# Fused cross-attention and FFN with LoRA on one core: the 4-byte passes of a head pair gathered into one group

## The reference

```python
def attention(hidden_q, hidden_kv, attention_mask, position_bias, Wq, Wk, Wv, Wo):
    q = (hidden_q @ Wq).reshape(b, lq, h, dh)      # b 16, lq 64, h 32, dh 128
    k = (hidden_kv @ Wk).reshape(b, lk, h, dh)
    v = (hidden_kv @ Wv).reshape(b, lk, h, dh)
    score = einsum('bqhd,bkhd->bhqk', q, k) * dh ** -0.5 + position_bias
    probs = softmax(where(mask, score, -inf)); probs = where(mask, probs, 0)
    return einsum('bhqk,bkhd->bqhd', probs, v).reshape(b, lq, h * dh) @ Wo
def ffn(x, ...):
    base_out = x @ base_W.T + base_b
    p = softmax(x @ router_W.T + router_b); w = the 8 largest of 15, summed by expert
    return base_out + (((x @ A.T) * w) @ B.T) * 2.0
x = x + attention(layernorm(x), ctx, mask, bias, Wq, Wk, Wv, Wo)
x = x + ffn(layernorm(x), ...)
```

## Time and profile before

| | |
|---|---|
| median of three runs | 833.14 us |
| profiled execution | 832.47 us |
| its span | 830.7 us |
| TensorE busy | 803.3 us, 97% |
| VectorE busy | 582.0 us, 70% |
| ScalarE busy | 341.0 us, 41% |
| GpSimd busy | 232.3 us, 28% |
| chain that ended last | TensorE 88%, VectorE 6% |

### The profile page before, as it was taken

How to read it: one execution, slowest core, us unless ns; L and a number is a source line. 1 busy time by engine, 2 the same in 40 slices (tenths; PEclk the granted TensorE clock), 3 DMA queues, 4 the chain that set the end, 5 groups by cost and what they waited for, 6 DMA issues and landing times.

```text
span 830.7 us, 16317 instructions
## 1 busy us (share of the span) xinstructions
PE 803.3 (97%) x6366; PEld 652.7 (79%) x6366; DVE 582.0 (70%) x1023; ACT 341.0 (41%) x657; POOL 232.3 (28%) x227
## 2 busy tenths in 40 slices
PE   8689999999999999969999999999999999998998
PEld 6578888888888888758888878888887878886786
DVE  4674435347677665588788888788787888758872
ACT  4544435245565554444334433344334433333410
POOL 0050404113424333253133322333133322111340
PEclk9789999999999999999999999999999999999999
DMA  6335665334454546564553436443563435442002
GB/s 215 99 142 169 231 224 178 114 130 163 153 177 153 176 148 203 193 188 135 153 176 112 141 108 179 134 145 106 152 178 112 137 110 152 122 150 38 1 9 93
DMA packets 108075, 118.35 MB, mean 142 GB/s; under 512 B 44240, under 2 KB 77008, under 8 KB 107999
## 3 DMA queue, kind: packets, MB, share of 16 engines
q1 hardware_dynamic: 107998, 117.31, 44.9%
HBM read 81.64 MB, written 35.65 MB: 141 GB/s over the span
## 4 chain that ended last, share of the span: by engine, by line
PE 88%; DVE 6%; ACT 2%; issue 1%; DMA 1%; POOL 0%; SPq 0%; ACTq 0%; DVEq 0%; POOLq 0%
PE pP L1253 38%; PE pY L1253 37%; PE pO L1433 4%; PE pS L1408 4%; PE pO L1253 2%; PE pT_ L1418 2%; DMA wk_raw<-in_L_xattn_Wq 1%; ACT wv_hi L624 1%; DVE co_lo L843 1%; PE pS L1299 1%; DVE oT_lo L843 0%; PE pT_ L1299 0%; DVE wk_lo L843 0%; DVE sums_c L887 0%; PE pO L1299 0%
## 5 line engine op out<-in xcount | busy, mean ns | idle before, releaser
L1063 DVE TENSOR_TENSOR y<-y,pY 128x512 f32<-128x512 f32 x124 | 84.4, 681 | 41.2 <-PE pY L1253 41.0
L1253 PE MATMUL pY<-wo_hi,oT_hi 128*128 128x512 f32 x248 | 97.8, 394 | 2.4 <-DVE y L1063 2.4
L1253 PE MATMUL pP<-xo_hi,wk_hi 128*128 128x512 f32 x224 | 97.2, 434 | 2.6 <-DVE q L853 1.7
L843 DVE TENSOR_TENSOR wk_lo<-twk,wk_hi 128x256 fp32r<-128x256 f32 x128 | 80.8, 643 | 23.7 <-ACT wk_hi L624 23.7
L1253 PE MATMUL pY<-wo_lo,oT_hi 128*128 128x512 f32 x248 | 96.8, 390 | 0.0
L1253 PE MATMUL pY<-wo_hi,oT_lo 128*128 128x512 f32 x248 | 96.5, 389 | 0.0
L1253 PE MATMUL pP<-xo_lo,wk_hi 128*128 128x512 f32 x224 | 88.7, 396 | 0.0
L1253 PE MATMUL pP<-xo_hi,wk_lo 128*128 128x512 f32 x224 | 88.4, 394 | 0.0
L547 POOL TENSOR_TENSOR bias<-bias,madd 128x512 f32<-128x512 f32 x32 | 42.0, 1313 | 139.5 <-DMA bias<-in_fside_Bx32xSxS 139.5
L624 ACT CAST wk_hi<-twk 128x256 fp32r<-128x256 f32 x128 | 52.1, 408 | 56.2 <-PE pP L1253 45.3
L843 DVE TENSOR_TENSOR wk_lo<-wk_raw,wk_hi 128x256 fp32r<-128x256 f32 x96 | 53.1, 553 | 20.9 <-ACT wk_hi L624 20.7
(11 more groups left out here) (256 smaller groups left out, 1887.5 us busy)
## 6 DMA issues: line engine op xcount, KB each, us to landing
v_hbm<-stage SPq DMA_DIRECT2D x64, 256.0 KB, 2.3
k_hbm<-stage SPq DMA_DIRECT2D x64, 256.0 KB, 3.2
k<-k_hbm SPq DMA_DIRECT2D x16, 1024.0 KB, 5.3
v<-v_hbm SPq DMA_DIRECT2D x16, 1024.0 KB, 6.1
wk_raw<-in_L_xattn_Wk SPq DMA_DIRECT2D x16, 512.0 KB, 4.5
wo_raw<-in_L_xattn_Wo SPq DMA_DIRECT2D x16, 512.0 KB, 3.7
bias<-in_fside_Bx32xSxS SPq DMA_DIRECT2D x128, 64.0 KB, 2.7
wk_raw<-in_L_xattn_Wq SPq DMA_DIRECT2D x16, 512.0 KB, 4.3
```

What stands on the lines that cost most here:

```text
L843: nc.vector.tensor_tensor(dst, src, hi.bitcast(F32), ALU.subtract).then_inc(done, 1)
L1063: nc.vector.tensor_tensor(y[:, t, :], y[:, t, :], src[:, :], ALU.add).then_inc(y_added, 1)
L1253: mm = nc.tensor.matmul(bank_, a, b, start=first and n == 0, stop=last and n == len(terms) - 1, skip_group_check=read_between)
```

## The change

TensorE's 4-byte passes of a pair stand together, once per pair: the transpositions of both heads of pair i, the scores of both heads of pair i+1, the products with V of pair i. The seven products and the eight Wo tiles follow; these are now of pair i itself, and the Q block is that of pair i+2. For that

- scores go into pY instead of pS, the two heads' transposed weights into pT_ and pS, and V's product of the second head into the same two banks; pT, the maxima, sums and reciprocals get a second copy; subtraction and exp work in place in `pr`; oT has one copy instead of two;
- K's last block and Q's first change places: Q's first is block 31 (`Q0`), K's last block 32; the scores of pair 0 stand inside block 32, and block 33 runs in the order of the first stage without any passes of a pair;
- the queues of all engines are written anew to this order, SyncE's with k ahead of both biases; k and v change places in SBUF;
- in the last turns, a_raw and the router's weights are fetched earlier and the FFN's transpositions stand in another order.

```diff
+Q0 = NV + NK - 1
 QA = NV + NK
+def is_q(n):
+    return n == Q0 or n > QA
...
-        pT = at("pT", R4 + 12288, [P, NT, S])
+        pT = [at("pT0", R4 + 12288, [P, NT, S]), at("pT1", R4 + 6144, [P, NT, S])]
...
+        pT_of = [pT_, pS]
+        pO_of = [pO, [pT_, pS]]
...
 # SyncE
-            for i in range(4):
-                sp.wait_ge(put[1][i], 16 * QA // 2)
-            load_v(0)
-            load_wk(22)
+            load_wk(QA - 10)
+            store(QA, 0, c11_made)
+            sp.wait_ge(s_full, 2)
+            load_k(1)
...
+            load_wk(QA - 9)
+            store(QA, 2, c21_made)
...
+            for i in range(4):
+                sp.wait_ge(put[0][i], 16 * (QA // 2 + 1))
+            load_v(0)
+            for i in range(NP - 1):
+                sp.wait_ge(wo_l, i + 1)
+                load_wo(i + 1)
+                if i + 2 < NP:
+                    sp.wait_ge(s_full, 2 * i + 4)
+                    load_k(i + 2)
+                    for s in range(2):
+                        sp.wait_ge(s_read, 2 * i + 3 + s)
+                        load_bias(2 * i + 4 + s)
+                if i + 24 < NSET:
+                    load_wk(i + 24)
+                sp.wait_ge(o_full, 4 * (i + 1))
+                load_v(i + 1)
...
 # ScalarE, per pair
+                turned_p(h); turned_p(h + 1); o_high(h); o_high(h + 1); copy_p1(n)
+                exp(h + 2); higher_of(w, 0); exp(h + 3); higher_of(w, 1); copy_u(n)
+                higher_of(w, 2); higher_of(w, 3); wo_high(i + 1); copy_v(n)
+                higher_of(w, 4); copy_c12(n); higher_of(w, 5); higher_of(w, 6)
...
 # VectorE, per pair
+                biased(h + 2); largest(h + 2); biased(h + 3)
+                less_max(h + 2); largest(h + 3); less_max(h + 3)
+                o_low(h, 0); o_low(h, 1); o_low(h + 1, 0); o_low(h + 1, 1)
+                lower_of(w, 0); make_c11(n); lower_of(w, 1)
+                add_up(h + 2); weights(h + 2); lower_of(w, 2); lower_of(w, 3)
+                add_tile(i, 0); add_up(h + 3); add_tile(i, 1); weights(h + 3)
+                make_c22(n); add_tile(i, 2); lower_of(w, 4); add_tile(i, 3)
+                lower_of(w, 5); add_tile(i, 4); add_tile(i, 5); make_c21(n)
+                add_tile(i, 6); lower_of(w, 6); add_tile(i, 7)
...
 # TensorE
+            times(n, 1); times(n - 1, 3); times(n, 2); times(n - 1, 4); times(n, 6)   # n = QA
+            scores(0); scores(1)
...
+            for i in range(NP - 2):
+                turn_p(h); turn_p(h + 1)
+                scores(h + 2); scores(h + 3)
+                times_v(h); times_v(h + 1)
+                for p in (1, 2, 6, 7):
+                    times(n, p)
+                times_wo(i, 0); times_wo(i, 1); times(n, 5)
+                times_wo(i, 2); times_wo(i, 3); times(n, 3)
+                times_wo(i, 4); times_wo(i, 5); times(n, 4)
+                times_wo(i, 6); times_wo(i, 7)
+            # i = NP - 2
+            turn_p(h); turn_p(h + 1); scores(h + 2); times_v(h); times_v(h + 1); scores(h + 3)
+            ffn_weights(0); ffn_weights(1)
+            for t in range(4):
+                times_wo(i, t)
+            ffn_weights(2); ffn_weights(3); times_wo(i, 4); times_wo(i, 5); ffn_weights(4)
+            times_wo(i, 6); times_wo(i, 7); turn_p(h + 2); turn_p(h + 3); ffn_weights(5)
+            times_v(h + 2); times_v(h + 3); ffn_weights(6)
```

More of the change, by code:

```diff
@@ new lines, in _ @@
+            n, w, late = QA, next_set(QA), late_set(QA)
+            copy_p1(n)
+            higher(w, 0)
+            copy_c12(n - 1)
+            higher(late, 5)
+            higher(w, 1)
+            higher(late, 6)
+            copy_u(n)
+            higher(w, 2)
+            exp(0)
+            higher(w, 3)
+            copy_v(n)
+            higher(w, 4)
+            copy_c12(n)
+            higher(w, 5)
+            exp(1)
+            higher(w, 6)
+            n, w = QA + 1, next_set(QA + 1)
@@ new lines, in _ @@
+            n, w, late = QA, next_set(QA), late_set(QA)
+            lower_w(w, 0)
+            lower_w(late, 5)
+            make_c11(n)
+            lower_w(w, 1)
+            make_c21(n - 1)
+            lower_w(late, 6)
+            biased(0)
+            lower_w(w, 2)
+            largest(0)
+            biased(1)
+            less_max(0)
+            largest(1)
+            lower_w(w, 3)
+            less_max(1)
+            make_c22(n)
+            lower_w(w, 4)
+            add_up(0)
+            lower_w(w, 5)
@@ new lines, in _ @@
+            make_c21(n)
+            n, w2 = QA + 1, next_set(QA + 1)
+            weights(0)
+            lower_w(w, 6)
+            lower_w(w2, 0)
+            make_c11(n)
+            add_up(1)
+            lower_w(w2, 1)
+            weights(1)
+            lower_w(w2, 2)
+            lower_w(w2, 3)
+            make_c22(n)
+            lower_w(w2, 4)
+            lower_w(w2, 5)
+            make_c21(n)
+            lower_w(w2, 6)
+            for i in range(NP - 2):
+                n = QA + 2 + i
@@ L1509, in _ @@
+            times(n, 1)
+            times(n - 1, 3)
+            times(n, 2)
+            times(n - 1, 4)
+            times(n, 6)
+            scores(0)
+            scores(1)
+            for p in (7, 5, 3, 4):
+                times(n, p)
+            for p in (1, 2, 6, 7, 5, 3, 4):
+                times(n + 1, p)
+            for i in range(NP - 2):
+                n = QA + 2 + i
+                h = 2 * i
                 turn_p(h)
-                times(n, 6)
-                times_wo(i - 1, 3)
+                turn_p(h + 1)
+                scores(h + 2)
+                scores(h + 3)
@@ L1541, in _ @@
[L1541 to L1543 removed]
+            times_wo(i, 4)
+            times_wo(i, 5)
+            ffn_weights(4)
+            times_wo(i, 6)
+            times_wo(i, 7)
+            turn_p(h + 2)
+            turn_p(h + 3)
+            ffn_weights(5)
+            times_v(h + 2)
+            times_v(h + 3)
+            ffn_weights(6)
             def turn_last(t):
```

547 lines of the change are left out of this document (250 added, 297 removed).

## The result

The changed kernel takes 845.93 us (median of 4 runs, 840.63 to 848.01) against 832.31 of the kernel before beside it: ratio 1.0141, 95% interval [1.0112, 1.017] (the two medians alone give 1.0164). Run once more later (x12): 840.62 us, ratio 1.0094 [1.007, 1.0118]. Neither interval holds 1. The forecast was 839, slower, case C; 845.93 lies inside the stated 815 to 847, but 0.9 above case C's own 832 to 845, and 840.62 lies inside both.

What follows compares the result with a forecast made beforehand. TensorE was taken to set the pace in the steady stage. Pairs +13.5, head -7.0 and last pair -0.5 gave +6.0 on the profiled 832.47 us, 838.5; with the runs' median 0.7 higher, 839, range 815 to 847.

Steps and rivals of the forecast that it cites:

- case C: The forecast itself: pairs lose more to waits than the group saves; 839 us, own range 832 to 845, chance 0.50.
- The mechanism: Pairs: late masks and lower_wo on GpSimd hold VectorE's two-SBUF-operand work, so Wo 2 and Wo 3 wait for additions.
- the bias can't land before k: Loads in the pairs: one ring's descriptors go in order, so bias behind k lands after 8.5; first mask addition taken at 9.4.
- Waits per turn: Pairs: TensorE waits 1.1 to 1.7 us at Wo 2, another 0.4 at Wo 3; sum 1.5 to 2.4, taken as 1.9.
- D: Rival, worse: c11 and lower 3 both late, or a lowered clock, or the head keeps its hole; 848 us, chance 0.13.
- What the group saves: Pairs: gathered 4-byte passes take 5.45 us against 6.27, saving 0.82 per pair (0.73 to 0.90).
- c11's slack: Pairs: VectorE's c11 is ready just before product 7 wants it at 9.6; no wait, 0.1 us of slack.
- Pairs in sum: 13 pairs at +1.1 us each and the 14th at -0.8: +13.5 us.
- Head: Start of the pair stage, up to 400 us: the hole and lowered clock go; -7.0 us, between 0 and -8.4.
- Last pair: End of the pair stage: the 1.84 us stall loses its cause, other waits come; -0.5 us, from -2.5 to +1.5.
- A: Rival: in the pairs no two-operand work stands behind lower_wo before tile 0; turn 25.8, 814 us, chance 0.22.
- B: Rival: k doesn't hinder, masks come ahead of lower 0, c11 slips and product 7 waits; turn 26.8, 826 us, chance 0.15.

Runs made afterwards that it cites:

- x12: The changed kernel, unedited, run once more: 840.62 us, ratio 1.0094 to the kernel before.
- x6: Changed kernel with only GpSimd's mask addition cut to 1 block and 8 columns (mask left out of nearly all scores): 816.77 us, ratio 0.9793.
- x3: Changed kernel with ScalarE's cast of Wo's high part for the next pair behind cast 5, so lower_wo starts later: 819.28 us, ratio 0.9836.
- x7: Changed kernel with VectorE's additions of Wo tiles 0 and 1 ahead of lowerings 2 and 3: 820.25 us, ratio 0.9835.
- x1: Changed kernel with GpSimd's mask addition and, from the third pair on, its lowering of Wo cut to a small part (outputs wrong): 815.94 us, ratio 0.9797.
- x10: Changed kernel with the moves of x3 and x7, c11 ahead of lowering 0, and Wo's cast for the last pair later: 812.47 us, ratio 0.9764.
- x9: Kernel before with the load of Wq's columns for block 33 right behind k instead of behind v: 831.53 us, ratio 0.9979.
- x4: Changed kernel with SP issuing the even head's bias, then k, then the odd head's bias: 826.35 us, ratio 0.9923.
- x11: x4 with VectorE making c11 ahead of lowering 0: 816.56 us, ratio 0.9808.

## Why the prediction was right, and which term was too small

- **The mechanism**: right, in each link (SP's k, late masks, small product, lowerings 2 and 3 behind lower_wo, tile 0, Wo 2 and 3). x6 (masks), x3 (lower_wo) and x7 (VectorE's order) break the chain at three places and x1 at two of them together, and each gains 20 us or more against either median of the kernel after. That the bias can't land before k holds for what the addition waits for: the fourth transfer of a head's bias landed behind k in all 15 cases of the first execution. The first of the four the profile puts ahead of k in five of them (in turn 5, 5.3 us after an issue at 507.51, k 6.5 us after 507.10), but it tells transfers apart only by the count of landings, so that is not certain.
- **Waits per turn**: forecast 1.9. Measured as the turn after minus that of x1: 28.01 - 26.12 = 1.89, and 2.11 in x12. The forecast's 1.1 to 1.7 at Wo 2 and 0.4 more at Wo 3 are both there, the first somewhat longer: in nine of 13 turns Wo 2 comes 1.3 to 2.1 us late, and Wo 3 another 0.3 to 0.4 where the clock is full (as in the lines at 579.20). That the mean hits 1.9 is in part luck. Turn by turn the difference to x1 goes from 0.5 (turns 6, 8 and 11, which hardly wait) to 3.9; a usual waiting turn loses 2.3 (turns 2, 4, 7 and 12), the upper end of the forecast's 1.5 to 2.4. Two turns of each execution had a lowered clock (below), some 0.25 of the 1.89, which the prediction had priced under D.
- **What the group saves**: forecast 0.82, measured 26.64 - 26.12 = 0.52, and this is the term that was mis-sized, by two things that go opposite ways. The group itself is shorter than forecast: 509.02 - 504.01 + 0.11 = 5.1 instead of 5.45: both scores take 2.01 to the start of V (504.98 to 506.99) where 2.16 and a turn of 0.08 were put, and V 2.03 where 2.18 was. The 1.08 that one head's scores take alone already hold the step on the way out (the last pass starts at 639.24, the product row at 639.39), and the forecast put it for each head; two heads on end pay it once, and so do the passes with V. That would save 1.1. But c11's slack, put at 0.1, was below zero. c11 came at its forecast time, 8.74 to 9.42 in turn 5, and it was product 7 that the shorter group made due at 9.2 instead of 9.6. It began at 9.57, in x1 too, with nothing of GpSimd in the way, and some 0.4 us are lost there. x10's c11 ahead of lowering 0 takes the undisturbed turn from 26.0 to 25.67. Against the 25.5 that 90 rows and 5.1 make, 0.1 is left at product 7 and the rest is rows that come a little slower than every 0.2264; the issue gaps below are in the means alone (25.89 in x10, 26.12 in x1). The Trainium skill's rule that a change of tiling mode drains the engine (TensorEngine Tiling (Array Packing), Key Properties) is borne out by the starts of single passes, between scores and V too: from the last score pass to the first of V it is 0.15 us (506.84 to 506.99), as it is from V to the product (508.87 to 509.02), where score passes come in pairs every 0.06; and from the last transposition to the scores 0.20, where transpositions come every 0.11.
- **Pairs in sum**: forecast +13.5; measured +17.1 and +20.1. From the turns of the first execution: 13 x (28.01 - 26.64) - 0.7.
- **Head**: forecast -7.0. From the marker to the first group 29.98 (364.08 - 334.10). Before, the point to compare with is 14 turns of 26.64 ahead of the last pair's scores at 744.87, so 371.91, and 371.91 - 330.42 = 41.49. Of the difference of 11.5, 2.9 (4-byte passes of the first pair, 2 x 0.36 + 2 x 1.09) only moved behind the first group: -8.6. No hole, clock 1.00: nearer to the end without waits. x9 shows that the hole's load was not worth the 6.3 that stood beside it: without it 1.65 come back, and the softmax of pair 0 was behind it.
- **Last pair**: forecast -0.5, measured -0.1: from group 14 to the end 90.44 against 832.47 - 744.87 = 87.60, less the same 2.9.
- **Sum**: +6.0 forecast, +8.5 and +11.5 measured from the marker; by medians +13.6 (first runs) and +7.5 (x12). Direction and range held, the range by 1.1 us. The pairs cost 3.6 to 6.6 more than forecast, and 1.6 of that came back in the head. Of the 13.6 of the first runs, 3.7 is the late start that their profiled execution shows, and up to 1 that the four executions of the kernel before were quicker (832.31) than in the later series (832.92 to 833.28); what the other executions did in the pairs no trace shows.
- **Rivals**: A is what x1 or x6 gives (forecast 814, measured 815.94 and 816.77, at turns of 26.1 and 26.25, not 25.8). B is x4 (826 forecast, 826.35 measured), but that agreement is luck: the turn is 27.2, not 26.8, and the 14 turns take 6.6 us more than before where B had 0.5 more. What decided between them and C was the k load and where lower 3 stood, as said. The rule of SBUF — State Buffer, Who interferes with whom, in the Trainium skill (VectorE with two SBUF inputs contends with a GpSimd instruction that reads SBUF) is borne out by x4: 1.48 for a lowering of 0.42 beside the mask addition. That an operation with one operand in PSUM is not held, x11 shows.

## What to carry to other kernels

Ask of each long operation of GpSimd which two-operand operation of VectorE it can meet, and what TensorE wait stands behind that one in VectorE's list; a collision that costs nothing in one order (26.64 a turn, with and without it) costs TensorE 2.3 us in a usual waiting turn of another. When passes are gathered into one group, the spacing that they gave to the softmax and to c11 goes with them, so list every result whose slack was that spacing, and count it against the shortest group that is possible: here the group's own gain used up c11's slack. A stall that hangs on such a chain can be broken at its cheapest link, here a few lines of order, and the saving that the change was made for then comes out: 812.5 against 832.9, of which 10.2 are in the 14 turns (372.96 to 362.73); about as much comes from the head and the last pairs.

## What was not expected of the hardware

- **The clock.** Turns 5 and 10 of both executions of the kernel after, and no other, ran at a mean clock of 0.94: 0.8 to 1.5 us behind the wait at Wo 2 rows come every 0.43 us instead of 0.23 (523.13 to 523.56), 1.2 instead of 2.4 GHz for some 3.4 us, which costs about 1.6. The waits at Wo 2 there were 1.79 and 1.75 in the first execution, 1.87 and 1.92 in the second; 1.89 and 1.92 in turns 1 and 4 of the second left the clock at 1.00. What picks these two is open. Of the second execution:

```profile
498.43:528.21 29.78, 27.72 (x292) 22.49 (x291) 23.46 (x36) 9.81 (x20) 8.27 (x8) 0.94 0.42 125
641.24:671.28 30.04, 27.93 (x291) 22.48 (x290) 23.52 (x36) 9.80 (x20) 8.26 (x8) 0.94 0.43 124
```

- **Gaps without a cause in the profile.** In the kernel before TensorE has none in 13 turns. With the group it has one of up to 1.2 us in or just behind the V passes, mostly in turns 0, 3, 6, 9 and 12, in every version. The longest is 1.17, in x6, at 600.90; a part of such a gap is not lost, since product 7 then waits less for c11. The group has some 200 short passes in 5 us; whether that is the cause was not tried.
- **VectorE gets in between two operations of GpSimd, and then holds the second.** The second mask addition took 1.73 instead of 1.29: it started at 515.91, when VectorE's product of the weights had run for 0.1 us of its 0.69 (515.80). Lowering 2 waited for the end of that addition (517.64) and ran there, ahead of lower_wo, which took 2.56 instead of 2.40; lowering 3 then waited for lower_wo. In turn 7 the held product of the weights did the same, and lower_wo took 2.83.
